# Moving splits of x, a swap of keys and a sum of absolute weights in a fused attention and ternary FFN kernel

## Chip, cores and metric

One core of a Trainium2 chip. The metric is the device time of one execution in microseconds (us). Everything below is fp32 data, multiplied on TensorE as pairs of reduced-precision parts.

## Reference

```python
# x (8, 512, 1024), cond_1 (8, 1), Wq, Wk, Wv, Wo, weight (1024, 1024), bias (1024)
q, k, v = x @ Wq.T, x @ Wk.T, x @ Wv.T            # 16 heads of 64
q = q * min(cond_1, 4)                            # one factor for each batch
attn = softmax(causal(q @ k.T / 8))
y = (attn @ v).reshape(8, 512, 1024) @ Wo.T
alpha = max(mean(abs(weight)), 1e-5)
q_w = clip(round(weight / alpha), -1, 1) * alpha  # ternary weight
scale = max(max(abs(y), axis=-1), 1e-5) / 127
q_y = clip(round(y / scale), -128, 127) * scale
out = x + q_y @ q_w.T + bias
```

## The kernel before

Every fp32 operand of a product is split in a high part (rounded by ScalarE's copy to the matmul's fp32r) and a low part (raw minus high, a subtraction on VectorE or GpSimd), and a product is three matmuls. `x_high` and `x_low` do that for a slice `k` (of 8) of the transposed x of a batch, 128x512 each; `pt_high` and `pt_low` for transposed probabilities; `xv_split`, `v_high` and `v_low` in the value stage.

The program has three stages. In the **value stage** (`v_pe`, `v_act`, `v_dve`, `v_pool`, `v_sp`) the values of all batches are computed and stored in DRAM: two plain iterations and then 14 iterations `n` = 2 to 15 of seven products each (A11, S4, A12, S2, S1, S3, A22; a Strassen-like form with sums of the blocks B11, B12, B21, B22 made on GpSimd by `xv_sums`). The same stage sums the absolute values of the FFN weight: `wf_abs(act, k)` for k = 0 to 7, two slices in each of the iterations 3 to 6, each loaded by SyncE (`load_wf`, L931) one iteration earlier. v_sum 0 on VectorE adds A12's bank to a copy of A11's; PE's product S1 waits for it (`v_product`).

In the **attention stage** 32 steps (4 groups of 4 heads, 8 batches) each project k and q of one batch (`project`, L174; projection `gi` = k0, q0, k1, q1, in 8 slices of 3 matmuls) and carry the attention of 16 units, a unit `u` being 128 queries of a head. The steps overlap: a step (`now`) begins the units 0 to 5 of its own batch and finishes 6 to 15 of the batch before (`old`), while x of the next one (`nxt`) is loaded. The order on each engine is written out by hand in `pe_step`, `act_step`, `dve_step`, `pool_step` and `sp_step`; each engine runs its list in order and waits on semaphores. A unit goes: scores (PE, L242 with `k_sw` and L243 with `k_st`), mask_max (VectorE, L254), exponent (ScalarE, L261), reciprocal (VectorE, L267), normalise (GpSimd, L273), transpose (PE, L283), `pt_high` (ScalarE, L297), `pt_low` (VectorE, L304), product with v (PE, L317). The transpose of unit u waits for `pt_low` of unit u - 2, since there are two banks; scores of unit u wait for mask_max of u - 2.

```python
            S(6); T(3); J(0, 0, 1)      # S scores, T transpose, J(projection, slices)
            S(7); T(4); J(0, 2, 3)
            S(8); T(5); J(0, 4, 5)
            PV(0); J(0, 6)
            S(9); T(6); J(0, 7)
```

That is the beginning of `pe_step` (the last slice of the step before is `J(3, 7)`, whose q is then evacuated by ScalarE, L204, and VectorE, L219). Slice k of the projection needs `x_lo` of that slice. The slices 0 to 3 of `nxt` are split at the end of a step and 4 to 7 at the beginning of the following one.

Scores need the keys twice, once with the partition halves exchanged. `swap_k(sp, it, blk)` makes `k_sw` by two SBUF to SBUF DMAs (L229, L230) for a block of two heads; block 0 is used by the scores 0 to 7, block 1 by 8 to 15. SyncE's list also holds the loads of x (`load_x`, L349, which waits until all `x_low` of the buffer are done), of the weights (`load_w`, L388, in three steps), of v (`load_v`, L381) and the stores of the attention output (`store_o`, L341).

In three steps (`qk_for`) the next group's q and k weights are loaded and split, the last quarter in the step after (`late_for`). The **output stage** then does the output projection, the quantisation and the ternary product for 32 tiles.

Of the kernel before, what the change touches and what calls it, by code (L numbers as in the profile page):

```python
# [36 lines left out]
def adaln_ffn_kernel(nc, x, xT, cond, wq, wk, wv, wo, wf, bias, out):  # L37
# [4 lines left out]
    with ExitStack() as ctx:  # L42
# [309 lines left out]
        def x_high(act, it, k):  # L352
            if k % 2 == 0:
                act.wait_ge(x_in[k // 2], (it + 1) * 16)
            if isinstance(it, int) and it == 0:
                act.wait_ge(v_product_done, V_LAST + 3)
            if due(count := (it - 1) * KT + k + 1):
                act.wait_ge(x_free, count)
            act.activation(x_hi[:, k, :], x_raw[:, k, :], ACT.Copy).then_inc(x_hi_done, 1)  # L359
# [566 lines left out]
        WF_ABS_FROM, WF_FROM = 3, 7  # L926
# [6 lines left out]
        def wf_abs(act, k):  # L933
            if not 0 <= k < KT:
                return
            act.wait_ge(wf_in[k % 2], (k // 2 + 1) * 16)
            act.activation(wf_tmp[k % 2], wf_tmp[k % 2], ACT.Abs, accum_out=wf_sums[:, k:k + 1])\
               .then_inc(wf_abs_done, 1)
# [91 lines left out]
        def v_act(act):  # L1030
            load_wv(act, 0)
            for i, (k0, k1) in enumerate(V_PIECES):
                if i == 0:
                    xv_split_plain(act, 0, 0, 0, False)
                    xv_split_plain(act, 0, 0, 1, False)
                if i == 2:
                    xv_split_plain(act, 0, 1, 0, False)
                    xv_split_plain(act, 0, 1, 1, False)
                act.wait_ge(wv_in[i], 16 * (k1 - k0))
                for k in range(k0, k1):  # L1040
                    wv_split(act, k, False)
            xv_split_plain(act, 1, 0, 0, False)
            xv_split_plain(act, 1, 1, 0, False)
            xv_split_plain(act, 1, 0, 1, False)
            xv_split_plain(act, 1, 1, 1, False)
            for q in range(4):
                v_high(act, 0, q)
            ws_high(act, S4)
            ws_high(act, S2)
            ws_high(act, S1)  # L1050
            xv_split(act, 2, B11, False)
            xv_split(act, 2, B22, False)
            for q in range(2):
                v_high(act, 1, q)
            xv_split(act, 2, B21, False)
            xv_split(act, 2, T2, False)
            v_high(act, 1, 2)
            xv_split(act, 2, T1, False)
            ws_high(act, S3)
            v_high(act, 1, 3)  # L1060
            xv_split(act, 2, T3, False)
            xv_split(act, 2, T4, False)
            for n in range(PLAIN, PAIRS):
                v_copy(act, n, V_TMP_A)
                xv_split(act, n + 1, B11, False)
                if n == PAIRS - 1:
                    for gi in range(4):
                        split_w_qk(act, -1, 0, gi, False)
                xv_split(act, n + 1, B22, False)
                xv_split(act, n + 1, B21, False)  # L1070
                v_high(act, n, 0)
                v_copy(act, n, V_TMP_U)
                if n == PAIRS - 1:
                    for k in range(4):
                        x_high(act, 0, k)
                xv_split(act, n + 1, T2, False)
                wf_abs(act, 2 * (n - WF_ABS_FROM))
                v_copy(act, n, V_TMP_R)
                if n == PAIRS - 1:
                    for k in range(4, KT):  # L1080
                        x_high(act, 0, k)
                xv_split(act, n + 1, T1, False)
                xv_split(act, n + 1, T3, False)
                wf_abs(act, 2 * (n - WF_ABS_FROM) + 1)
                v_high(act, n, 1)
                v_high(act, n, 2)
                v_copy(act, n, V_TMP_P)
                xv_split(act, n + 1, T4, False)
                v_high(act, n, 3)
# [198 lines left out]
        def act_step(act, old, now, nxt, qk_for=None, late_for=None, last=False):  # L1288
            o, n, x = old and old[0], now and now[0], nxt and nxt[0]
            ending = last and not now  # L1290

            def E(u):
                if u >= 5 and old:
                    exponent(act, o, u)
                elif u < 5 and now:
                    exponent(act, n, u)

            def H(u):
                if u >= 2 and old:
                    pt_high(act, o, u)  # L1300
                elif u < 2 and now:
                    pt_high(act, n, u)

            def V(gi):
                if now:
                    evac_hi(act, n, gi)

            def OL(h):
                if old:
                    o_lower(act, o, h)  # L1310

            def X(*ks):
                if nxt:
                    for k in ks:
                        x_high(act, x, k)

            def W(gi):
                if qk_for is not None:
                    split_w_qk(act, n, qk_for, gi, False)

            def WO(k):
                if ending:
                    wo_high(act, k)

            H(2)
            if old:
                evac_hi(act, o, 3)
            WO(2)
            if now and old:
                x_high(act, n, 4)  # L1330
            E(5)
            if now and old:
                x_high(act, n, 5)
            WO(3)
            H(3)
            E(6)
            if now and old:
                x_high(act, n, 6)
            if late_for is not None:
                split_w_qk(act, o, late_for, 3, False)  # L1340
            WO(4)
            H(4)
            E(7)
            if now and old:
                x_high(act, n, 7)
            H(5)
            E(8)
            OL(0)
            WO(5)
            H(6)  # L1350
            V(0)
            E(9)
            WO(6)
            H(7)
            E(10)
            H(8)
            E(11)
            WO(7)
            H(9)
            E(12)  # L1360
            OL(1)
            H(10)
            V(1)
            E(13)
            H(11)
            E(14)
            W(0)
            H(12)
            E(15)
            H(13)  # L1370
            E(0)
            OL(2)
            H(14)
            V(2)
            E(1)
            W(1)
            H(15)
            E(2)
            X(0, 1)
            if last and now:  # L1380
                o_high(act, 0, 0)
                wo_high(act, 0)
            W(2)
            H(0)
            E(3)
            X(2, 3)
            if last and now:
                wo_high(act, 1)
            H(1)
            E(4)  # L1390
            OL(3)
            if last and now:
                o_high(act, 1, 1)

        def dve_step(dve, old, now, nxt, qk_for=None, late_for=None, last=False):
# [48 lines left out]
            M(6)  # L1444
            if now and old:
                x_low(dve, n, 4)
            WO(2)
            L(3)
            I(6)
            M(7)  # L1450
            if now and old:
                x_low(dve, n, 6)
            WO(3)
            if late_for is not None:
                split_w_qk(dve, o, late_for, 3, True)
# [65 lines left out]
        def pool_step(pool, old, now, nxt, qk_for=None, late_for=None, last=False):  # L1521
            o, n, x = old and old[0], now and now[0], nxt and nxt[0]
            ending = last and not now
            for u in range(5, UNITS):
                if old:
                    normalise(pool, o, u)
                if now and old and u in (5, 7):
                    x_low(pool, n, u)
            if ending:
                split_o(pool, 2, 0)  # L1530
            if now:
                for u in range(5):
                    normalise(pool, n, u)
                    if nxt and 2 <= u < 4:
                        x_low(pool, x, 2 * u - 3)
                    if last and u == 3:
                        o_low_part(pool, 0, 0)
                if last:
                    o_low_part(pool, 1, 1)

        def sp_step(sp, old, now, nxt, qk_for=None, late_for=None, last=False):
            ending = last and not now
            if nxt and old:
                load_x(sp, *nxt)
            if qk_for is not None:
# [29 lines left out]
                load_x(sp, *nxt)  # L1575
            if now:
                load_v(sp, *now, 2)
                swap_k(sp, now[0], 1)
            if now:
                load_v(sp, *now, 3)  # L1580
            if last and now:
# [136 lines left out]
```

## Time and profile before

| | |
|---|---|
| time, median of 3 runs | 2057.48 us (2057.24 to 2062.15) |
| time of the profiled execution | 2057.48 us |
| its span, first to last instruction | 2055.7 us |
| mean granted TensorE clock | 0.996 |
| busy: TensorE matmul, VectorE, ScalarE, GpSimd | 97%, 69%, 54%, 42% |
| value stage, attention stage, output stage | to about 337, to about 1575, to the end |
| a plain attention step | 38.0 us |

PE is TensorE's matmul, PEld its weight load, DVE VectorE, ACT ScalarE, POOL GpSimd, SP SyncE (SPq its queue). In a timeline, a row is the start, the time, the engine, the line, the operation and its tiles, a count, and in brackets the idle time before it with what ended it. The start-to-start distance of two rows of an engine is shorter than the duration of the first when they are pipelined.

### The profile page before, as it was taken

Reading aid. Unit: us, or ns where it says so; the run is one execution under the profiler, and the core shown is the slowest. Engines: PE = TensorE matmul, PEld = TensorE weight load, DVE = VectorE, ACT = ScalarE, POOL = GpSimd, SP = SyncE. Lnnn points to the kernel's source line nnn. Section 1 sums busy time; section 2 is a strip of 40 time slices with the busy share of each in tenths; the row PEclk is TensorE's granted clock in tenths of the full one; section 3 lists DMA queues with packets and bytes.
Section 4 is the critical chain, followed back from the end, with each engine's and each line's share of the span. In section 5 each row is a group of like instructions: output and inputs, shape, how many; then the busy total and the mean of one; then the engine's idle time right before and its main releaser. Section 6 shows DMA issues by size and latency. Waiting matters only on the chain.

```text
span 2055.7 us, 34723 instructions
## 1 busy us (share of the span) xinstructions
PE 1988.6 (97%) x10074; PEld 1619.1 (79%) x10074; DVE 1411.2 (69%) x3277; ACT 1115.7 (54%) x2497; POOL 872.2 (42%) x816
## 2 busy tenths in 40 slices
PE   8999999999999999999999999999998999999998
PEld 6888887888877888877888877888886777777775
DVE  6667776777777777778777777777776645545454
ACT  4554445777777777777777777777774000000000
POOL 0344333444435444435445435445443544444442
PEclk9999999999999999999999999999999999999999
DMA  6676645533543533543533543533553432333322
GB/s 204 225 232 219 203 170 183 156 112 114 141 149 103 159 107 105 155 148 103 151 115 102 158 149 103 154 112 102 158 153 101 130 120 94 107 108 100 114 92 82
DMA packets 200981, 282.43 MB, mean 137 GB/s; under 512 B 11216, under 2 KB 146384, under 8 KB 199760
## 3 DMA queue, kind: packets, MB, share of 16 engines
q1 hardware_dynamic: 200384, 281.07, 44.9%
q8 instruction: 34, 0.56, 0.1%
q10 hardware_dynamic: 528, 0.52, 0.1%
q14 instruction: 35, 0.29, 0.0%
HBM read 178.79 MB, written 69.21 MB: 121 GB/s over the span
## 4 chain that ended last, share of the span: by engine, by line
PE 47%; issue 27%; POOL 15%; DVE 5%; DMA 3%; ACT 2%; SPq 1%; POOLq 1%; DVEq 0%; ACTq 0%
POOL prob L273 9%; PE proj_ps L508 8%; PE s_ps L508 8%; PE t_ps L869 7%; PE proj_ps L174 6%; PE o_ps L869 6%; POOL parts L365 5%; PE o_ps L579 5%; DMA k_sw<-k_st 2%; PE o_ps L317 1%; PE t_ps L283 1%; DVE prob L254 1%; DVE parts L365 1%; PE t_ps L557 1%; PE s_ps L808 1%
## 5 line engine op out<-in xcount | busy, mean ns | idle before, releaser
L174 PE MATMUL proj_ps<-parts 128*128 128x512 f32 x3072 | 839.2, 407 | 6.0 <-POOL parts L365 3.6
L273 POOL TENSOR_TENSOR prob<-prob,row_inv 128x128 f32<-128x128 f32 (+3 forms) x512 | 383.1, 748 | 693.5 <-DVE row_inv L267 690.9
L174 PEld LDWEIGHTS proj_ps<-parts 128*128 128x128 f32 x3072 | 538.8, 189 | 112.1 <-POOL parts L365 13.3
L261 ACT ACTIVATE prob<-prob,row_min 128x128 f32<-128x128 f32 (+3 forms) x512 | 287.5, 561 | 145.8 <-DVE row_min L254 139.5
L254 DVE CUSTOM_DVE_ANT_0 prob<-s_ps,mask 128x128 f32<-128x128 f32 (+3 forms) x512 | 248.2, 485 | 56.5 <-PE s_ps L243 22.1
L297 ACT ACTIVATE pt_hi<-t_ps 128x128 fp32r<-128x128 f32 (+3 forms) x512 | 220.7, 431 | 112.2 <-PE t_ps L283 108.2
L564 ACT ACTIVATE yt_q<-t_ps 128x1024 bf16<-128x1024 bf16 x32 | 32.7, 1023 | 427.1 <-PE t_ps L557 427.1
L304 DVE TENSOR_TENSOR pt_lo<-t_ps,pt_hi 128x128 fp32r<-128x128 f32 (+3 forms) x512 | 249.0, 486 | 16.7 <-ACT pt_hi L297 12.5
L283 PE MATMUL t_ps<-ident,prob 128*128 128x128 f32 x1280 | 227.4, 276 | 31.9 <-DVE pt_lo L304 29.4
L365 POOL TENSOR_TENSOR parts<-x_raw,parts 128x512 fp32r<-128x512 f32 x128 | 183.4, 1434 | 18.1 <-ACT parts L359 18.1
L508 PE MATMUL proj_ps<-parts,o_parts 128*128 128x512 f32 x768 | 188.2, 400 | 2.6 <-issue 2.6
L283 PEld LDWEIGHTS t_ps<-ident,prob 128*128 128x128 f32 x1280 | 152.7, 141 | 47.5 <-issue 34.2
L508 PE MATMUL s_ps<-parts,o_parts 128*128 128x512 f32 x768 | 185.6, 397 | 0.0
L508 PEld LDWEIGHTS proj_ps<-parts,o_parts 128*128 128x128 f32 x768 | 143.7, 190 | 33.6 <-issue 3.0
L508 PEld LDWEIGHTS s_ps<-parts,o_parts 128*128 128x128 f32 x768 | 143.2, 189 | 30.7
L243 PE MATMUL s_ps<-k_st,q_st 128*128 128x128 f32 (+3 forms) x512 | 166.0, 324 | 0.0
L242 PE MATMUL s_ps<-k_sw,q_st 128*128 128x128 f32 (+3 forms) x512 | 158.3, 309 | 7.2 <-DMA k_sw<-k_st 7.0
L317 PE MATMUL o_ps<-pt_lo,v_st 128*128 128x512 f32 (+3 forms) x512 | 161.6, 326 | 2.7 <-DVE pt_lo L304 2.7
L359 ACT ACTIVATE parts<-x_raw 128x512 fp32r<-128x512 f32 x256 | 152.0, 618 | 3.1 <-DMA x_raw<-xT 2.2
L317 PE MATMUL o_ps<-pt_hi,v_st 128*128 128x512 f32 (+3 forms) x512 | 147.7, 325 | 0.0
L267 DVE RECIPROCAL row_inv<-row_sum 128x1 f32<-128x1 f32 x512 | 82.5, 161 | 92.9 <-ACT prob L261 85.6
L334 DVE TENSOR_TENSOR o_sum<-o_ps,o_low 64x512 f32<-64x512 f32 x128 | 87.4, 683 | 82.6 <-ACT o_low L326 82.5
(118 smaller groups left out, 2880.3 us busy)
## 6 DMA issues: line engine op xcount, KB each, us to landing
x_raw<-xT SPq DMA_DIRECT2D x128, 512.0 KB, 5.7
v_scratch<-v_out SPq DMA_DIRECT2D x64, 512.0 KB, 3.3
k_sw<-k_st SPq DMA_DIRECT2D x128, 256.0 KB, 4.7
v_st<-v_scratch SPq DMA_DIRECT2D x128, 256.0 KB, 4.2
oT_scratch<-o_sum SPq DMA_DIRECT2D x64, 256.0 KB, 2.5
x_raw<-oT_scratch SPq DMA_DIRECT2D x32, 512.0 KB, 4.8
x_tile<-x SPq DMA_DIRECT2D x32, 512.0 KB, 5.4
out<-res SPq DMA_DIRECT2D x32, 512.0 KB, 3.2
```

What stands on the lines that cost most here:

```text
L174: mm = pe.matmul(out, l, r, start=(k == 0 and i == 0), stop=(k == KT - 1 and i == 2))
L243: pe.matmul(s_ps[u % 2][:, 0:w], q, k_st[:, h, 0:w], start=False, stop=True).then_inc(s_done, 1)
L254: dve.tensor_tensor_reduce(prob[:, u % 4, 0:w], s_ps[u % 2][:, 0:w], mask[:, S - w:S], 1.0, -MASKED, ALU.add, ALU.min, row_min[:, u % 4:u ...
L261: act.activation(prob[:, u % 4, 0:w], prob[:, u % 4, 0:w], ACT.Exp, bias=row_min[:, u % 4:u % 4 + 1], scale=-1.0, accum_out=row_sum[:, u % ...
L273: pool.tensor_tensor(prob[:, u % 4, 0:w], prob[:, u % 4, 0:w], row_inv[:, u % 4:u % 4 + 1].broadcast_to([P, w]), ALU.mult).then_inc(norm_d ...
L283: mm = pe.transpose(t_ps[u % 2][:, kb * P:(kb + 1) * P], prob[:, u % 4, kb * P:(kb + 1) * P], ident[:, :])
L297: act.activation(pt_view(pt_hi[h % 2], qt), t_ps[u % 2][:, 0:(qt + 1) * P] .rearrange("p (k q) -> p k q", q=P), ACT.Copy).then_inc(pt_hi_d ...
L304: dve.tensor_tensor(pt_view(pt_lo[h % 2], qt), t_ps[u % 2][:, 0:(qt + 1) * P] .rearrange("p (k q) -> p k q", q=P), pt_view(pt_hi[h % 2], q ...
L317: mm = pe.matmul(o_ps[h % 2][:, q0:S], v, part[h % 2][:, kb, q0:S], start=(kb == 0 and part is pt_lo), stop=(kb == QT - 1 and part is pt_hi))
L365: eng.tensor_tensor(x_lo[:, k, :], x_raw[:, k, :], x_hi[:, k, :].bitcast(F32), ALU.subtract).then_inc(x_lo_done[k % 2], 1)
L508: mm = pe.matmul(y_ps[p][half][:, :], a[p][:, o], b[k][:, w], start=(k == 0 and i == 0), stop=(k == KT - 1 and i == 2))
L869: mm = pe.matmul(bank[:, :], xv[:, c, xp, ks], wv_view(c, wp)[:, k, :], start=(k == 0 and m == 0 and c not in (S2, S3)), stop=(k == CH - 1 ...
```

## The change

In the value stage, the even slice's `wf_abs` moves on ScalarE's list from after the split of T2 to after the split of B11. In a step, on ScalarE `x_high` 5 moves ahead of exponent 5, and 6 and 7 to right after it; on VectorE `x_low` 6 moves from after mask_max 7 to right after `x_low` 4; on GpSimd `x_low` 5 moves ahead of normalise 5 and `x_low` 7 ahead of normalise 6; on SyncE the swap of key block 1 moves from between two loads of v to the head of the next step.

```diff
@@ v_act
                 v_copy(act, n, V_TMP_A)
                 xv_split(act, n + 1, B11, False)
+                wf_abs(act, 2 * (n - WF_ABS_FROM))
...
                 xv_split(act, n + 1, T2, False)
-                wf_abs(act, 2 * (n - WF_ABS_FROM))
                 v_copy(act, n, V_TMP_R)
@@ act_step
             if now and old:
                 x_high(act, n, 4)
+                x_high(act, n, 5)
             E(5)
             if now and old:
-                x_high(act, n, 5)
+                x_high(act, n, 6)
+                x_high(act, n, 7)
             WO(3)
             H(3)
             E(6)
-            if now and old:
-                x_high(act, n, 6)
             if late_for is not None:
                 split_w_qk(act, o, late_for, 3, False)
             WO(4)
             H(4)
             E(7)
-            if now and old:
-                x_high(act, n, 7)
             H(5)
@@ dve_step
             M(6)
             if now and old:
                 x_low(dve, n, 4)
+                x_low(dve, n, 6)
             WO(2)
             L(3)
             I(6)
             M(7)
-            if now and old:
-                x_low(dve, n, 6)
@@ pool_step
+            if now and old:
+                x_low(pool, n, 5)
             for u in range(5, UNITS):
                 if old:
                     normalise(pool, o, u)
-                if now and old and u in (5, 7):
-                    x_low(pool, n, u)
+                if u == 5 and now and old:
+                    x_low(pool, n, 7)
@@ sp_step
             ending = last and not now
+            if old:
+                swap_k(sp, old[0], 1)
             if nxt and old:
                 load_x(sp, *nxt)
...
             if now:
                 load_v(sp, *now, 2)
-                swap_k(sp, now[0], 1)
             if now:
                 load_v(sp, *now, 3)
```

(`E` is an exponent, `H` a `pt_high`, `L` a `pt_low`, `M` a mask_max, `I` a reciprocal; `WO` is for the last step alone.)

## Rows read from the trace of the kernel before

**Rows 1.** The page, part 1: busy us, share of the span, instructions.

```profile
PE 1988.6 (97%) x10074; PEld 1619.1 (79%) x10074; DVE 1411.2 (69%) x3277; ACT 1115.7 (54%) x2497; POOL 872.2 (42%) x816
```

**Rows 2.** The list of waits: who waited for whom, us in total, times, longest.

```profile
PE t_ps L283 <- DVE pt_lo L304: 29.4, 35, 2.8
...
PEld proj_ps L174 <- POOL parts L365: 13.3, 31, 1.4
...
PE s_ps L242 <- DMA k_sw<-k_st: 7.0, 3, 2.4
```

**Rows 3.** Timeline of PE, the beginning of a plain step (scores 8, transpose 5).

```profile
814.36 0.23 PE L242 MATMUL s_ps<-k_sw,q_st 128*128 128x128 f32 x1
...
815.56 0.41 PE L283 MATMUL t_ps<-ident,prob 128*128 128x128 f32 x2 [0.86 <-DVE pt_lo L304]
```

**Rows 4.** Timeline of ACT, the same step.

```profile
812.00 0.63 ACT L359 ACTIVATE parts<-x_raw 128x512 fp32r<-128x512 f32 x1
812.54 0.49 ACT L261 ACTIVATE prob<-prob,row_min 128x256 f32<-128x256 f32 x1
...
813.03 0.61 ACT L359 ACTIVATE parts<-x_raw 128x512 fp32r<-128x512 f32 x1
```

**Rows 5.** Timeline of DVE, the same step.

```profile
813.36 0.16 DVE L267 RECIPROCAL row_inv<-row_sum 128x1 f32<-128x1 f32 x1
813.64 0.56 DVE L254 CUSTOM_DVE_ANT_0 prob<-s_ps,mask 128x384 f32<-128x384 f32 x1
...
814.12 0.69 DVE L365 TENSOR_TENSOR parts<-x_raw,parts 128x512 fp32r<-128x512 f32 x1
814.73 0.68 DVE L304 TENSOR_TENSOR pt_lo<-t_ps,pt_hi 128x512 fp32r<-128x512 f32 x1
```

**Rows 6.** Timeline of POOL, the same step.

```profile
813.60 0.61 POOL L273 TENSOR_TENSOR prob<-prob,row_inv 128x256 f32<-128x256 f32 x1 [2.21 <-DVE row_inv L267]
814.17 1.78 POOL L365 TENSOR_TENSOR parts<-x_raw,parts 128x512 fp32r<-128x512 f32 x1
...
818.63 1.28 POOL L365 TENSOR_TENSOR parts<-x_raw,parts 128x512 fp32r<-128x512 f32 x1
```

**Rows 7.** Timeline of all engines, value stage, iteration 4.

```profile
103.30 1.74 POOL L796 TENSOR_TENSOR xv_raw<-xv_raw 128x512 f32<-128x512 f32 x1
103.81 1.77 DVE L920 TENSOR_TENSOR v_out<-v_tmp,v_out 128x512 fp32r<-128x512 f32 x1
```

**Rows 8.** Timeline of SP's queue, the end of the step before.

```profile
803.30 0.47 SPq L229 DMA_DIRECT2D k_sw<-k_st  x1
...
810.83 0.37 SPq L341 DMA_DIRECT2D oT_scratch<-o_sum  x1
```

**Rows 9.** Transfers into `k_sw` issued from 803 to 806 us.

```profile
DMA to landing us min/median/max: 3.1/3.4/3.7
```

**Rows 10.** Timeline of PE, scores 0 of a step that loads weights.

```profile
603.51 0.33 PE L242 MATMUL s_ps<-k_sw,q_st 128*128 128x128 f32 x1 [2.40 <-DMA k_sw<-k_st]
```

**Rows 11.** Busy time by windows: engines' busy us (instructions), granted clock, DMA share, GB/s.

```profile
604.80:608.10 3.30, 3.30 (x15) 3.01 (x13) 1.07 (x3) 0.79 (x3) 0.40 (x2) 0.50 0.27 78
...
1200.00:1300.00 100.00, 93.59 (x502) 78.91 (x501) 76.65 (x207) 73.42 (x174) 44.15 (x51) 1.00 0.51 150
```

**Rows 12.** Timeline of SP's queue, value stage, iterations 4 and 5.

```profile
100.99 1.26 SPq L931 DMA_DIRECT2D x_raw<-wf  x2
...
118.01 1.26 SPq L931 DMA_DIRECT2D x_raw<-wf  x2
```

**Rows 13.** The first of each of these pairs: issue to landing.

```profile
DMA to landing us min/median/max: 5.8/5.8/5.8
...
DMA to landing us min/median/max: 4.8/4.8/4.8
```

**Rows 14.** Timeline of ACT, iteration 5: `wf_abs` of slice 4.

```profile
124.90 1.05 ACT L937 ACTIVATE x_raw<-x_raw 128x1024 f32<-128x1024 f32 x1
```

**Rows 15.** Timeline of DVE, iteration 5: v_sum 0.

```profile
121.17 0.69 DVE L898 TENSOR_TENSOR v_tmp<-t_ps,v_tmp 128x512 f32<-128x512 f32 x1 [0.64 <-PE t_ps L869]
```

**Rows 16.** Timeline of PE, iteration 5: product S1.

```profile
123.69 2.88 PE L869 MATMUL t_ps<-wv_last,xv 128*128 128x512 f32 x12
```

## Prediction

> **What bounds the kernel now.** The page comes first: TensorE is busy 97% of the span and no other engine above 79% [rows 1]. So the time is PE's matmul time plus its gaps, and an edit off PE matters only if it opens or closes a gap. The list of PE's waits says which gaps exist: 35 waits for a `pt_lo` (29.4 us) and three for a landed `k_sw` (7.0 us); the weight loads of the projection also wait 31 times, 13.3 us in all, for an `x_low` of GpSimd [rows 2]. The timeline of a plain step, read engine by engine, says where the first kind sits. Scores 8 run at 814.36, then PE idles 0.86 us until transpose 5 at 815.56 [rows 3]. Transpose 5 waits for `pt_low` of unit 3, which on DVE starts at 814.73 and lasts 0.68, so ends at 815.41 [rows 5]. In front of it stand the reciprocal of unit 5 (813.36), mask_max 6 (813.64) and `x_low` 4 (814.12). PE reaches scores 8 regardless, so whatever is put in front of `pt_low` 3 adds to that gap one for one. There are 31 such steps.
>
> **The change in a step.** No instruction is added or removed; five kinds are moved.
>
> ScalarE. Now `x_high` 4 (812.00), exponent 5 (812.54), `x_high` 5 (813.03) [rows 4]. After: 4, 5, exponent 5, 6, 7, then `pt_high` 3. One `x_high` holds ScalarE 0.54 (812.54 less 812.00). Exponent 5 starts near 813.08, and its sum, ready at about 813.1 now, is ready at 813.6. The reciprocal 5 on DVE goes from 813.36 to about 813.70 (it had 0.3 of slack), mask_max 6 to 813.98, and `x_low` 4, 0.48 after that, would start at 814.45. `pt_high` 3 moves by about 1.0 and ends near 815.2, which is not what comes last.
>
> GpSimd. `x_low` 5 now runs ahead of normalise 5. `x_high` 5 would end at 813.15, so it runs 813.2 to 814.5: 1.28 is its undisturbed length, at 818.63; the one at 814.17 took 1.78 because it started 0.05 after DVE's `x_low` 4 and waited for it [rows 6, 5]. Normalise 5 (0.61) then stands ready at 814.5 and `x_low` 7 behind it.
>
> VectorE. `x_low` 6 is moved in front of `pt_low` 3. Alone it costs 0.61 (814.73 less 814.12). But these subtractions read two SBUF operands, and the trace shows that they and GpSimd's take turns. DVE's subtraction at 103.81 took 1.77, and it ends with a GpSimd operation ahead of it; GpSimd's at 103.30 took 1.74, behind another of DVE [rows 7]. Each waiter got its turn before the other engine's next instruction. So after: GpSimd holds until 814.5, DVE `x_low` 4 to 815.1, normalise 5 to 815.65, DVE `x_low` 6 to 816.2, and only then `pt_low` 3 to 816.85 and transpose 5 at 817.0. That is 1.45 later than 815.56: a gap of 2.3 us instead of 0.86. Bounds: without any turn-taking `pt_low` 3 starts at 814.45 + 2 x 0.61 = 815.67, transpose 5 at 816.5 (+0.95). If GpSimd's normalise 5 gets its turn before `x_low` 4, a matter of 0.05 us at 814.5, then `x_low` 7 (1.28) also comes in between and transpose 5 runs at 818.3 (+2.7). I take the middle, since DVE arrives at 814.45 and GpSimd's next instruction cannot arrive before its first is over. In the Trainium skill, "SBUF — State Buffer", section "SBUF: two separate sides", this port pair is an exclusive lock held for a whole instruction, which speaks against putting the two subtractions next to each other; with the lock the row's +1.45 follows, without it +0.95.
>
> SyncE. The swap of the second key block now stands after `store_o`, at the head of the next step. The store is issued at 810.83; with 0.37 for it and a loop branch the two swaps go out at about 811.65 and 812.15 instead of 803.30 [rows 8]. In flight beside little else they land 3.1 to 3.7 after issue [rows 9], so near 815.9. Scores 8 (now 814.36) must wait for that: a second new wait of 1.6, inside the 2.3 of the first. It costs nothing as long as `pt_low` 3 is later, and is a floor: were DVE's part free, transpose 5 would still come at about 816.2 (+0.6). Behind the swap on that queue stands the load of the next x, which waits for `x_low` 7 anyway. In the first step the swap goes out at its old time, and in the last one matmuls of the output projection stand before scores 8; both nothing.
>
> What is given back. `x_low` 7 now ends by about 817.5 (818.63 + 1.28 = 819.9 before), so projection slice 7 no longer waits on it. Those are the 31 waits of 13.3 us, the longest 1.4 [rows 2]: about 0.4 a step. Net of a step 1.45 - 0.43 = 1.02, times 31 = +32. The next x is loaded some 2.4 us earlier, and in the three steps that also load weights scores 0 waits for a `k_sw` queued behind those bytes (2.40 at 603.51; 7.0 in all [rows 2, 10]); these waits go: -7.0.
>
> **TensorE's clock.** After the wait of 2.40 at 603.51 the granted clock was 0.50 (1.2 GHz) in 604.80 to 608.10 and 1.00 (2.4 GHz) later: 3.3 us at half speed lose 1.65. The third wait of this kind was followed by none (1.00 over 1200 to 1300), the second by one, and the gaps of 0.86 by none [rows 11]. So a stall of 2.3 is where it can go either way. Two of three is the row's rate; as a delayed step shifts the next one, a run of steps may fall on either side. I take 25 of 31: +41; bounds none and all (+51). Two such stretches go with the `k_sw` waits: -3.3. In the Trainium skill, "TensorE: Matmul & The Clock Gate", section "HAM oscillation — how this bites in real kernels", only idle gaps longer than all of these are to be avoided; by it the +41 would be 0. The row at 603.51 disagrees.
>
> **The change in the value stage.** In iterations 3 to 6 the even `wf_abs` moves ahead of the split of B22. Its input is issued at 118.01 in iteration 5 and lands 4.8 later, at 122.8 [rows 12, 13]; now it is used at 124.90 [rows 14], so it never waits. After, ScalarE reaches it at about 117.8 and stands until 122.8; the Abs holds it 1.1, the split of B22 0.6, DVE's low part 0.65 and v_sum 0.6. DVE's list has B22's low part before v_sum 0, now done at 121.17 + 0.69 [rows 15]. PE's product S1 needs v_sum 0: it can start at 125.85, its place is 123.69 [rows 16]: +2.2. Iterations 3 and 6 read alike (2.5, 2.2). In iteration 4 the input is issued at 100.99 and lands at 106.8 [rows 12, 13]; Abs to v_sum brings S1 to 109.8 against a place of 104.6, itself 2.5 later by then, and the load slips by about 1: +3.7. Sum +10.6, plus two half-clock stretches, 3.3: +14. Bounds 8 (other work absorbs some) and 20.
>
> **Sum.** 32 - 7.0 + 41 - 3.3 + 14 = +77. The profiled execution took 2057.48, 1.8 more than its span of 2055.7, and is also the median. Forecast 2135.
>
> **Rivals.**
> (a) The stalls come but the clock hardly falls, or the stall is the shorter one. For: one `k_sw` wait of three, and all gaps of 0.86, were followed by no fall. With +1.02 a step: 32 - 7 - 3.3 + 11 = +33, 2090. With transpose 5 only 0.95 later, 31 x 0.52 = 16, so +17, 2074. The skill's clock rule above would bring this case about.
> (b) GpSimd gets its turn first: 2.7 - 0.4 = 2.3 a step, 71, with a half-clock stretch in nearly every step (51): 71 - 10 + 51 + 14 = +126, 2183. It needs DVE to arrive 0.05 later than I read.
> (c) Faster. The mechanism is the freeing of `x_low` 7 alone: 13 + 7.0 + 3.3 = 23 gained. It decides if `pt_low` 3 starts no more than 0.3 later, that is by 815.05, and the value stage costs under 15: 2035 to 2050. Against it: exponent 5 alone is 0.5 later, `x_low` 6 costs at least 0.61, and the swap lands after scores 8's present time.
> (d) The step's parts and the refunds cancel, within 0.3%, that is within 6 us, about what a measurement of this kernel can tell from no change.
>
> **Chances.** Forecast (2105 to 2155) 0.45; (a) 0.30; (b) 0.12; (c) 0.08; (d) 0.05. The range runs from the lower end of (a), 2070, to 2168, between forecast and (b), and leaves out (c), (d) and most of (b). Forecast's own range 2105 to 2155. Faster 0.08, same 0.05, slower 0.87.
>
> **What would show it.** In a plain step: scores 8 waiting for `k_sw`; transpose 5 for `pt_lo` with a gap of about 2.3 in all; DVE `x_low` 6 about 1.2 long; slice 7 with no wait; the load of x near 817.7 + the step's shift; granted clock near 0.93 over the attention stage; no `k_sw` wait at scores 0. In the value stage, four waits of PE at S1. Wrong if the gap before transpose 5 stays under 1.2, if `x_low` 5 starts before `x_high` 5 could matter (GpSimd late for another reason), or if the clock stays at 1.00.

## Result and the profile after

The changed kernel takes 2133.93 us (median of 4 runs, 2132.82 to 2137.03) against 2058.89 before: a ratio of 1.0365, 95% interval 1.0347 to 1.0383, slower. The profiled execution took 2138.23, its span is 2136.4.

The page, part 1, of the kernel after, answers [rows 1].

```profile
PE 2029.9 (95%) x10074; PEld 1649.6 (77%) x10074; DVE 1411.3 (66%) x3277; ACT 1112.6 (52%) x2497; POOL 883.8 (41%) x816
```

The same matmuls are busy 41.3 us longer (2029.9 - 1988.6): that is the clock, as its record shows below. The rest of the longer span is PE's gaps, 106.5 us (2136.4 - 2029.9) against 67.1: +39.4. So half of the loss is waiting and half is slower matmuls. (The two profiled executions are 80.7 us apart, the medians 75.) The list of PE's waits after, against [rows 2]:

```profile
PE s_ps L242 <- DMA k_sw<-k_st: 46.4, 30, 2.1
PE t_ps L283 <- DVE pt_lo L304: 22.8, 36, 2.1
PE t_ps L869 <- DVE v_tmp L898: 12.2, 4, 3.4
```

It would be easy to read that the swap cost 46 us. Experiment 2 shows that in this kernel taking it back returns nothing. PE in a plain step, against [rows 3]:

```profile
857.65 0.32 PE L242 MATMUL s_ps<-k_sw,q_st 128*128 128x128 f32 x1 [1.55 <-DMA k_sw<-k_st]
...
858.46 0.41 PE L283 MATMUL t_ps<-ident,prob 128*128 128x128 f32 x2 [0.38 <-DVE pt_lo L304]
```

Two waits in a row, 1.93 together, where 0.86 stood. ScalarE in that step, against [rows 4]; the first row is the evacuation of q, from which both steps are measured below. Before, that row was:

```profile
810.58 1.39 ACT L204 ACTIVATE q_st<-proj_ps,q_scale 64x512 fp32r<-64x512 f32 x2 [0.17 <-PE proj_ps L174]
```

and now the step reads:

```profile
852.15 1.40 ACT L204 ACTIVATE q_st<-proj_ps,q_scale 64x512 fp32r<-64x512 f32 x2 [0.15 <-PE proj_ps L174]
853.57 1.15 ACT L359 ACTIVATE parts<-x_raw 128x512 fp32r<-128x512 f32 x2
854.63 0.49 ACT L261 ACTIVATE prob<-prob,row_min 128x256 f32<-128x256 f32 x1
...
855.12 1.14 ACT L359 ACTIVATE parts<-x_raw 128x512 fp32r<-128x512 f32 x2
856.28 0.60 ACT L297 ACTIVATE pt_hi<-t_ps 128x512 fp32r<-128x512 f32 x1
```

VectorE and GpSimd in the same step, against [rows 5, 6]:

```profile
855.52 0.56 DVE L254 CUSTOM_DVE_ANT_0 prob<-s_ps,mask 128x384 f32<-128x384 f32 x1
...
856.01 1.71 DVE L365 TENSOR_TENSOR parts<-x_raw,parts 128x512 fp32r<-128x512 f32 x2
857.64 0.68 DVE L304 TENSOR_TENSOR pt_lo<-t_ps,pt_hi 128x512 fp32r<-128x512 f32 x1
```

```profile
854.80 1.30 POOL L365 TENSOR_TENSOR parts<-x_raw,parts 128x512 fp32r<-128x512 f32 x1 [1.81 <-ACT parts L359]
856.06 1.11 POOL L273 TENSOR_TENSOR prob<-prob,row_inv 128x256 f32<-128x256 f32 x1
857.13 1.72 POOL L365 TENSOR_TENSOR parts<-x_raw,parts 128x512 fp32r<-128x512 f32 x1
```

The two `x_low` of VectorE take 1.71 instead of 2 x 0.61. Normalise 5 on GpSimd, 0.61 alone, takes 1.11: it waits for the first `x_low` and runs between the two. Measured from the evacuation of q (810.58 before, 852.15 after) transpose 5 moved from 4.98 to 6.31, +1.33.

Some of that is given back at slice 7 of the projection. Its first matmul started 0.58 after the first of the three transposes ahead of it, and starts 0.25 after it now, 0.33 less:

```profile
819.39 0.49 PE L283 MATMUL t_ps<-ident,prob 128*128 128x128 f32 x3
819.97 0.72 PE L174 MATMUL proj_ps<-parts 128*128 128x512 f32 x2
```

```profile
862.29 0.49 PE L283 MATMUL t_ps<-ident,prob 128*128 128x128 f32 x3
862.54 0.70 PE L174 MATMUL proj_ps<-parts 128*128 128x512 f32 x2
```

That leaves 1.00 a step. From scores 8 to scores 8 a plain step took 38.03 before (776.33 to 814.36), and takes 38.99 (857.65 to 896.64) where no fall of the clock follows:

```profile
776.33 0.22 PE L242 MATMUL s_ps<-k_sw,q_st 128*128 128x128 f32 x1
```

```profile
896.64 0.32 PE L242 MATMUL s_ps<-k_sw,q_st 128*128 128x128 f32 x1 [1.54 <-DMA k_sw<-k_st]
```

SyncE's queue at the end of the step before, against [rows 8]; the two swaps land 3.1 to 3.7 after issue, as in [rows 9]:

```profile
852.42 0.37 SPq L341 DMA_DIRECT2D oT_scratch<-o_sum  x1
853.20 0.47 SPq L229 DMA_DIRECT2D k_sw<-k_st  x1
853.72 0.59 SPq L230 DMA_DIRECT2D k_sw<-k_st  x1
```

If the second is the one that takes 3.7, it lands at 857.4, and scores 8 run at 857.65.

The granted clock by windows, against [rows 11]: behind the wait of one step (at 817.0) and behind that of the next (at 857.65).

```profile
819.30:822.50 3.20, 3.20 (x11) 2.81 (x10) 0.95 (x5) 0.86 (x4) 1.44 (x2) 0.50 0.79 253
...
858.90:862.20 3.30, 3.30 (x19) 2.83 (x19) 1.25 (x8) 2.17 (x6) 2.17 (x3) 1.00 0.53 134
```

In about as much time PE runs 11 matmuls at 0.50 (1.2 GHz) and 19 at 1.00 (2.4 GHz). The first step was followed by a fall, the next, with the same wait, was not; why one step is spared and another isn't stays open here. The trace's clock record has such a stretch, 3.4 us long, in 23 of the 31 steps, and one behind each of the four waits in the value stage. In all it has 31, where the one before has 6. The four waits of the value stage are, against [rows 16], in the rows of product S1:

```profile
88.64 4.58 PE L869 MATMUL t_ps<-wv_last,xv 128*128 128x512 f32 x12 [3.23 <-DVE v_tmp L898]
112.94 4.44 PE L869 MATMUL t_ps<-wv_last,xv 128*128 128x512 f32 x12 [3.39 <-DVE v_tmp L898]
137.00 4.37 PE L869 MATMUL t_ps<-wv_last,xv 128*128 128x512 f32 x12 [3.28 <-DVE v_tmp L898]
159.94 4.58 PE L869 MATMUL t_ps<-wv_last,xv 128*128 128x512 f32 x12 [2.25 <-DVE v_tmp L898]
```

The product that took 2.88 takes up to 4.58, half clock again. ScalarE in the third of these iterations shows the cause, against [rows 14]:

```profile
127.67 0.62 ACT L787 ACTIVATE xv<-xv_raw 128x512 fp32r<-128x512 f32 x1
133.86 1.06 ACT L937 ACTIVATE x_raw<-x_raw 128x1024 f32<-128x1024 f32 x1 [5.57 <-DMA x_raw<-wf]
```

ScalarE stands 5.57 us for the slice of the FFN weight, with the split of B22 behind it.

### The profile page after: what moved, and what is told of

Same layout as the page of the kernel before. It is cut to its first block, busy times and chain, and to the rows that moved or that the text cites. A ratio compares the mean times of both kernels' runs of the same rounds, so it can differ in the third digit from the quotient of the medians.

```text
span 2136.4 us, 34723 instructions
## 1 busy us (share of the span) xinstructions
PE 2029.9 (95%) x10074; PEld 1649.6 (77%) x10074; DVE 1411.3 (66%) x3277; ACT 1112.6 (52%) x2497; POOL 883.8 (41%) x816
## 4 chain that ended last, share of the span: by engine, by line
PE 70%; DVE 10%; issue 8%; ACT 8%; DMA 3%; ACTq 1%; DVEq 0%; SPq 0%; POOL 0%; POOLq 0%
PE proj_ps L174 23%; PE proj_ps L508 8%; PE s_ps L508 8%; PE o_ps L317 6%; PE t_ps L869 5%; PE o_ps L579 5%; PE t_ps L283 5%; PE o_ps L869 4%; ACT parts L359 3%; DVE parts L365 2%; PE s_ps L243 2%; PE s_ps L242 2%; DVE prob L254 2%; ACT prob L261 2%; DVE pt_lo L304 1%
## 5 line engine op out<-in xcount | busy, mean ns | idle before, releaser
L174 PE MATMUL proj_ps<-parts 128*128 128x512 f32 x3072 | 858.4, 414 | 0.0
L273 POOL TENSOR_TENSOR prob<-prob,row_inv 128x128 f32<-128x128 f32 (+3 forms) x512 | 397.0, 776 | 688.2 <-DVE row_inv L267 683.2
L174 PEld LDWEIGHTS proj_ps<-parts 128*128 128x128 f32 x3072 | 549.7, 193 | 101.7
L283 PE MATMUL t_ps<-ident,prob 128*128 128x128 f32 x1280 | 227.8, 276 | 25.5 <-DVE pt_lo L304 22.8
L242 PE MATMUL s_ps<-k_sw,q_st 128*128 128x128 f32 (+3 forms) x512 | 160.6, 314 | 46.6 <-DMA k_sw<-k_st 46.4
L317 PE MATMUL o_ps<-pt_lo,v_st 128*128 128x512 f32 (+3 forms) x512 | 172.1, 346 | 2.7 <-DVE pt_lo L304 2.7
L242 PEld LDWEIGHTS s_ps<-k_sw,q_st 128*128 128x128 f32 x512 | 96.5, 188 | 79.9 <-issue 47.0
L317 PE MATMUL o_ps<-pt_hi,v_st 128*128 128x512 f32 (+3 forms) x512 | 157.2, 343 | 0.0
```

Source lines behind the costliest of these rows:

```text
L174: mm = pe.matmul(out, l, r, start=(k == 0 and i == 0), stop=(k == KT - 1 and i == 2))
L242: pe.matmul(s_ps[u % 2][:, 0:w], q, k_sw[:, h, 0:w], start=True, stop=False)
L273: pool.tensor_tensor(prob[:, u % 4, 0:w], prob[:, u % 4, 0:w], row_inv[:, u % 4:u % 4 + 1].broadcast_to([P, w]), ALU.mult).then_inc(norm_d ...
L283: mm = pe.transpose(t_ps[u % 2][:, kb * P:(kb + 1) * P], prob[:, u % 4, kb * P:(kb + 1) * P], ident[:, :])
L317: mm = pe.matmul(o_ps[h % 2][:, q0:S], v, part[h % 2][:, kb, q0:S], start=(kb == 0 and part is pt_lo), stop=(kb == QT - 1 and part is pt_hi))
```

## Experiments

Each kernel was timed against before on the same chip (the medians of before were 2060.8 to 2062.1 there), so the ratio is what to compare. A difference in us is the ratio less one, times 2061.

**1. The parts, one at a time.** Three kernels with one part of the change each: the swap (SyncE), the Abs (value stage), the splits (ScalarE, VectorE, GpSimd).

```diff
# swap_only: sp_step
+            if old:
+                swap_k(sp, old[0], 1)
...
-                swap_k(sp, now[0], 1)
```

> Only SyncE's swap of key block 1 moves to the head of the next step; all else as before. The theory: the swap lands 1.55 us after PE has reached scores 8, so transpose 5 comes at about 0.65 us later than before (it had 0.86 of its own wait for pt_lo, which runs in parallel), 31 steps: +20 us; a gap of 1.5 is too short to bring the clock down: about 2079. The rival, that the wait for k_sw which the changed kernel's list of waits shows (46.4 us) is what the change cost: +46 us or more, 2105.

```diff
# abs_only: v_act
                 xv_split(act, n + 1, B11, False)
+                wf_abs(act, 2 * (n - WF_ABS_FROM))
...
-                wf_abs(act, 2 * (n - WF_ABS_FROM))
```

> Only the even wf_abs moves, in the value stage. The theory: ScalarE stands until the slice lands and PE waits at S1 in four iterations (12.2 us in the changed kernel), each followed by a stretch at half clock (4 x 1.65): +19 us, about 2078. The rival, that the stage has slack that takes it up later: under +6.

```diff
# splits_only: act_step, dve_step and pool_step as in the change
+                x_high(act, n, 5)
...
+                x_low(dve, n, 6)
...
+                x_low(pool, n, 5)
```

> Only the x_high and x_low moves on ScalarE, VectorE and GpSimd. The theory: pt_low 3 starts 1.3 later, the gap before transpose 5 is about 2.0 instead of 0.86 without any wait for k_sw; 31 x 1.1 = +34, half-clock stretches in about 23 steps +38, given back 13 (x_low 7) and 7 + 3.3 (k_sw at scores 0): +49, about 2107. The rival, that the swap was the last to come and the splits only stand in its shadow: about 2059 or less.

| | time | ratio (95%) | us |
|---|---|---|---|
| swap_only | 2079.02 | 1.0090 (1.0074 to 1.0107) | +19 |
| abs_only | 2078.29 | 1.0080 (1.0064 to 1.0097) | +16 |
| splits_only | 2115.77 | 1.0257 (1.0240 to 1.0274) | +53 |
| all three | 2133.93 | 1.0365 (1.0347 to 1.0383) | +75 |

The rivals fall, and the three totals are within 4 us of what was expected, but one of them by luck (swap_only, below). In abs_only the clock fell behind three of the four waits, not all four. The sum of the parts, 88, is 13 above the whole: two of them hide each other. PE in a plain step of swap_only:

```profile
864.07 0.32 PE L242 MATMUL s_ps<-k_sw,q_st 128*128 128x128 f32 x1 [1.53 <-DMA k_sw<-k_st]
...
864.35 0.40 PE L283 MATMUL t_ps<-ident,prob 128*128 128x128 f32 x2
```

Scores 8 wait 1.53 and the transpose then waits for nothing, since its `pt_lo` became ready meanwhile: the new wait of 1.53 swallows the old one of 0.86. A step is not 0.65 longer, as expected, but 0.44: 38.47 from the scores 8 before to these.

```profile
825.60 0.32 PE L242 MATMUL s_ps<-k_sw,q_st 128*128 128x128 f32 x1 [1.51 <-DMA k_sw<-k_st]
```

The clock, which was to stay up, fell behind four of the 31 steps. 31 x 0.44 = 14 and 4 x 1.65 = 7 make 21 where 31 x 0.65 = 20 was expected: two errors of opposite sign. The profiled execution was the fastest of four; the slowest took 2083.33 at a mean granted clock of 0.989 against 0.994.

In splits_only it is the other way round, one wait of 1.88 for `pt_lo`:

```profile
879.07 0.41 PE L283 MATMUL t_ps<-ident,prob 128*128 128x128 f32 x2 [1.88 <-DVE pt_lo L304]
```

**2. The whole without the swap.** The splits and the Abs of the change; the swap stays in its old place.

```diff
# after_old_swap: the changed kernel, sp_step
-            if old:
-                swap_k(sp, old[0], 1)
...
+                swap_k(sp, now[0], 1)
```

> The changed kernel with the swap back in its old place. The theory: the swap is hidden under the later pt_low 3, so almost nothing comes back: 2130, within 6 us of the changed kernel. The rival, that PE's waits for k_sw are the cost: 2085 or less.

2134.05, ratio 1.0348 (1.0331 to 1.0365): within 0.2% of the changed kernel, which the intervals can't tell from nothing. The wait of 46.4 us that the list names disappears, and the same time is listed for the other:

```profile
PE t_ps L283 <- DVE pt_lo L304: 70.1, 38, 3.0
PE t_ps L869 <- DVE v_tmp L898: 10.8, 4, 3.0
```

46.4 + 22.8 = 69.2 before this edit, 70.1 after it. A wait is charged to whatever is first in PE's order; what stands behind it doesn't show.

**3. Which of the splits.** VectorE's `x_low` 6 stays behind mask_max 7; ScalarE and GpSimd as in the change.

```diff
# act_pool_only against splits_only: dve_step
                 x_low(dve, n, 4)
-                x_low(dve, n, 6)
             WO(2)
             L(3)
             I(6)
             M(7)
+            if now and old:
+                x_low(dve, n, 6)
```

> The x_high and x_low moves on ScalarE and GpSimd alone; x_low 6 stays behind mask_max 7 on VectorE. The theory: pt_low 3 starts right after x_low 4, about 0.4 later than before, so the gap before transpose 5 is about 1.25, too short for a fall of the clock; 31 x 0.4 = +12, given back 13 and 10.3: about -11, 2051 where before takes 2062. The rival, that the x_high moves on ScalarE (pt_high 3 one us later) are what delays transpose 5: the gap stays near 2.0 and the time near that of splits_only, 2110 or more.

2055.80, ratio 0.9972 (0.9963 to 0.9982): a little faster than before, 6 us where 11 were expected, and 59 us faster than splits_only. The gap is now:

```profile
853.61 0.41 PE L283 MATMUL t_ps<-ident,prob 128*128 128x128 f32 x2 [1.17 <-DVE pt_lo L304]
```

and no step is followed by a fall of the clock. So the one `x_low` ahead of `pt_low` 3 carries the whole loss of the splits.

The 11 us expected had left out that ScalarE comes last now: with VectorE's second `x_low` out of the way, `pt_low` 3 waits about 0.2 for the later `pt_high` 3, in 29 of the 31 steps (6 us), which it did in none before:

```profile
852.77 0.69 DVE L304 TENSOR_TENSOR pt_lo<-t_ps,pt_hi 128x512 fp32r<-128x512 f32 x1 [0.22 <-ACT pt_hi L297]
```

**4. Turns between VectorE and GpSimd.** As splits_only, but GpSimd keeps its old order, so that `x_low` 5 and not normalise 5 stands ready between VectorE's two.

```diff
# pool_old against splits_only: pool_step
-            if now and old:
-                x_low(pool, n, 5)
             for u in range(5, UNITS):
                 if old:
                     normalise(pool, o, u)
-                if u == 5 and now and old:
-                    x_low(pool, n, 7)
+                if now and old and u in (5, 7):
+                    x_low(pool, n, u)
```

> As splits_only, but GpSimd keeps its old order: normalise 5, then x_low 5; x_low 7 after normalise 7. A test of the turns at the shared operands. The theory: between VectorE's x_low 4 and x_low 6 GpSimd now gets its turn with x_low 5 (1.28) instead of normalise 5 (0.61), so the pair takes about 2.4 instead of 1.71 and the gap before transpose 5 is about 2.6 instead of 1.93: 31 x 0.65 = 20 more, and the clock falls in two or three steps more (5): about 2140. The rival, that the two x_low merely cost their own 1.2 on VectorE: the pair takes 1.2 to 1.7 and the time is 2116 or less, as one operation less stands ahead on GpSimd.

2139.34, ratio 1.0385 (1.0368 to 1.0402), 26 us above splits_only. VectorE and GpSimd in a step of it:

```profile
848.45 2.36 DVE L365 TENSOR_TENSOR parts<-x_raw,parts 128x512 fp32r<-128x512 f32 x2
850.73 0.68 DVE L304 TENSOR_TENSOR pt_lo<-t_ps,pt_hi 128x512 fp32r<-128x512 f32 x1
```

```profile
847.93 0.62 POOL L273 TENSOR_TENSOR prob<-prob,row_inv 128x256 f32<-128x256 f32 x1 [2.51 <-DVE row_inv L267]
848.50 1.76 POOL L365 TENSOR_TENSOR parts<-x_raw,parts 128x512 fp32r<-128x512 f32 x1
```

The pair on VectorE grew from 1.70 in splits_only (1.71 in the changed kernel) to 2.36, and the operation between the two is 0.67 longer (1.28 against 0.61). In these kernels the length of the pair is set by what GpSimd has ready; the rival falls. The gap before transpose 5 is 2.53.

**5. Why the early Abs costs.** At the same early place stands the Abs of the odd slice loaded one iteration earlier.

```diff
# abs_landed: v_act
                 xv_split(act, n + 1, B11, False)
+                wf_abs(act, 2 * (n - WF_ABS_FROM) - 1)
...
-                wf_abs(act, 2 * (n - WF_ABS_FROM) + 1)
```

> Only the value stage: an Abs stands at the same early place, but it is that of the odd slice loaded one iteration earlier, which has landed; the even one stays late. The theory, that the cost of the early Abs is the wait for its input: no wait of PE at S1 and 2062, as before. The rival, that 1.1 us more of ScalarE ahead of the split of B22 is what costs: PE waits 1 us or more at S1 in four iterations, 2067 or more.

2060.25, ratio 0.9999 (0.9990 to 1.0009), and no wait of PE at S1. It isn't ScalarE's 1.1 us that costs, it is the transfer that it waits for.

**6. The queue behind the weights.**

```diff
# w_first against before: sp_step
+            if qk_for is not None:
+                load_w(sp, qk_for)
             if nxt and old:
                 load_x(sp, *nxt)
-            if qk_for is not None:
-                load_w(sp, qk_for)
```

> Before, with the loads of the q and k weights moved on SyncE's list ahead of the load of x in the three steps that have them. The theory: they start some 10 us earlier, the swap of key block 0 no longer queues behind them, and PE's three waits at scores 0 (7.0 us) and the two half-clock stretches behind them (3.3) go: 2052. The rival, that the bytes only move and another wait takes their place: 2060 to 2064.

2051.19, ratio 0.9950 (0.9934 to 0.9967): 10 us, as expected. But its timeline has a wait in these three steps that before didn't show:

```profile
611.60 0.41 PE L283 MATMUL t_ps<-ident,prob 128*128 128x128 f32 x2 [1.08 <-DVE pt_lo L304]
```

On VectorE a low split of the weights (1.26) stands in front of that `pt_low`:

```profile
609.60 1.26 DVE L398 TENSOR_TENSOR parts<-w_raw,parts 128x1024 fp32r<-128x1024 f32 x1
```

The wait of 2.40 at scores 0 had covered it. The changed kernel has the same rows (1.08, three times), where the wait at scores 0 went too.

**7. A version that beats both.** w_first, and in a step:

```diff
# best against w_first: pe_step, dve_step, act_step, pool_step
             T(5)
-            J(0, 4, 5)
             PV(0)
-            J(0, 6)
+            J(0, 4, 5, 6)
...
-                x_low(dve, n, 4)
...
             L(3)
+            if now and old:
+                x_low(dve, n, 4)
...
             H(4)
+            if now and old:
+                x_high(act, n, 7)
             E(7)
-            if now and old:
-                x_high(act, n, 7)
...
-                if now and old and u in (5, 7):
-                    x_low(pool, n, u)
+                if now and old and u in (5, 6):
+                    x_low(pool, n, 2 * u - 5)
```

> A version meant to beat both: w_first's order; the product with v of head 0 ahead of the projection slices 4 and 5 on PE, so that x_low 4 can stand behind pt_low 3 on VectorE; x_high 7 ahead of exponent 7 and x_low 7 ahead of normalise 7. The theory: the gap before transpose 5 halves (31 x 0.45 = 14), slice 7 doesn't wait (13), scores 0 doesn't wait (10): 2062 - 37 = 2025. The rival, that a delayed mask_max 7 or normalise makes a new wait of the same size: 2045 or more.

2028.25, ratio 0.9839 (0.9822 to 0.9855): 33 us faster than before (2025 was expected), 106 less than the changed kernel. The rival, a new wait of the same size, didn't come. PE in a plain step:

```profile
840.46 0.23 PE L242 MATMUL s_ps<-k_sw,q_st 128*128 128x128 f32 x1
...
841.23 0.41 PE L283 MATMUL t_ps<-ident,prob 128*128 128x128 f32 x2 [0.43 <-DVE pt_lo L304]
```

**The clock over all of these.** The number of the 31 attention steps in which the trace's clock record has a stretch at 0.50 behind the wait at scores 8 or transpose 5, beside that wait:

| kernel | wait in a plain step | steps followed by a fall |
|---|---|---|
| before | 0.86 | 0 |
| act_pool_only | 1.17 | 0 |
| swap_only | 1.53 | 4 |
| splits_only | 1.88 | 22 |
| after | 1.93 | 23 |
| pool_old | 2.53 | 29 |

## Why the prediction was right

- **What binds.** PE, with its gap before transpose 5 set by `pt_low` 3. Shown by experiments 1 and 3: with VectorE's second `x_low` (0.61 alone) out of the way the gap shrinks from 1.88 to 1.17.
- **ScalarE.** Exponent 5 was to be 0.5 later and `pt_high` 3 not last. After, `pt_high` 3 ends at 856.88 and `pt_low` 3 starts at 857.64. Right, with 0.76 to spare; without `x_low` 6 in the way `pt_high` 3 does come last, by 0.2 (experiment 3).
- **VectorE and GpSimd.** Forecast that the order of turns is subtraction, normalise 5, subtraction, and `pt_low` 3 +1.47. The rows show that order; transpose 5 came 1.33 later instead of 1.45. The prediction gave the three turns 0.6, 0.55 and 0.55, where its own rows had 0.61 each, without saying why; its 1.7 for the three is what they took (1.71). Experiment 4 changed the operation in between and the pair grew by the difference. Rival (b), GpSimd first, didn't come. The exclusive lock of the Trainium skill ("SBUF — State Buffer", section "SBUF: two separate sides") agrees with these rows, in which normalise 5 took 1.11 behind VectorE's `x_low`, and 0.61 alone.
- **The swap.** Forecast: scores 8 wait 1.6, nothing lost because `pt_low` 3 is later, a floor of +0.6 a step otherwise. Measured 1.55; experiment 2 shows the nothing. The floor was 0.44 in swap_only, whose +19 holds some falls of the clock as well.
- **Given back.** That the wait of slice 7 and those at scores 0 go: right, neither is in the list after. The weight loads' wait of 0.43 was worth 0.33 in PE's own starts. As both terms of a step were 0.1 too large, the net of 1.02 is nearly the measured 1.00 (0.96 from scores 8 to scores 8): that it fits so well is luck. And three waits of 1.08 behind the one at scores 0 (experiment 6) hadn't been seen: 3 of the 7 us were lost again.
- **Clock.** 25 of 31 steps were taken, 23 measured; four stretches in the value stage instead of two; two taken back. The net is 25 stretches x 1.65 = 41, and PE's busy time grew by 41.3; the forecast, 41 + 3.3 - 3.3, was 41. That a stall of this size can bring the clock down was read from rows and is right. That it would in 25 of 31 steps was not derived (two of three would be 21), for a stall of 2.3 that turned out 1.93: a choice that came near by luck, and it is why rival (a) had 0.30. One of its signs was wrong by its own sum: 41 us lost in some 1300 is a clock of 0.97, not 0.93, and 0.96 was measured over 337 to 1650. By the section of the Trainium skill that it names ("TensorE: Matmul & The Clock Gate", section "HAM oscillation — how this bites in real kernels") none of these stretches would have come; the 23 behind waits of 1.93 decide against that.
- **Value stage.** Waits of 10.6 were forecast, 12.2 measured (3.23, 3.39, 3.28, 2.25 against 2.5, 3.7, 2.2, 2.2). The iteration of 5.57 was mis-sized by 1.1, the others by less. Alone the part costs 16 against 14.
- **Sum.** PE's gaps 32 - 7 + 10.6 = 36 forecast, 39.4 measured; slower matmuls 41 and 41.3. Together 80.7 between the profiled executions; the total of +77 compares with a median difference of 75.

## What to carry over

When one operation has to go in front of the instruction that the bottleneck engine waits for, move it behind, even by one place. A list of waits charges each gap to one cause: before undoing the cause that it names, ask what would be late next; here the edit that had 46 us against its name was worth nothing as long as another stayed, which was worth nearly all of the steps' loss. A total that comes out as forecast doesn't prove its terms: look at the length of one step and count the falls of the clock. Price two neighbouring VectorE subtractions on SBUF operands with what GpSimd has ready between them (1.71 with normalise 5, 2.36 with an `x_low`, where the two alone take 1.22), and price a wait of an engine with the transfer behind it, not with the engine's own microsecond.

## What the hardware showed

A gap of PE that grows from 1.2 to 1.9 us, in a kernel that is otherwise dense, cost more in clock than in waiting. The number of steps followed by a fall went from none of 31 to 22, and each cost about another 1.65 us, so a growth of 0.7 us cost about 1.9 a step (59 us between act_pool_only and splits_only, over 31: 22 of waiting and 36 of clock).

VectorE and GpSimd took turns at subtractions and products with two SBUF operands: an operation that was ready on one engine ran before the next one of the other, and so came between two that stand next to each other in the other's list. With normalise 5 between, VectorE's pair of `x_low` took 1.71, with `x_low` 5 between, 2.36.
